# The guard, the input turns and the MLP's token shift of two windowed attention layers

## The reference

```python
def shift_token(t):                     # the second half of the features comes from the token before
    t1, t2 = jnp.split(t, 2, axis=-1)
    t2 = jnp.pad(t2, ((0, 0), (1, 0), (0, 0)))[:, :-1]
    return jnp.concatenate([t1, t2], axis=-1)
def l2norm(t):
    return t / jnp.clip(jnp.linalg.norm(t, axis=-1, keepdims=True), 1e-12)
def _layer(x, ...):
    q, k, v = split(shift_token(x) @ wqkv)            # 8 heads of 64
    q, k = rotary_xpos(l2norm(q) * qs, l2norm(k) * ksc)
    x = x + local_attention(q, k, v) @ wo             # windows of 64 tokens, each sees the one before too
    h = layernorm(shift_token(x)) @ w1 + b1
    a, g = jnp.split(h, 2, axis=-1)                   # 341 each
    return x + (a * gelu(g)) @ w2 + b2
```

## Time and profile before

| What | us |
|---|---|
| three executions | 1544.87, 1540.82, 1539.07; median 1540.82 |
| the profiled execution | 1543.41, its span 1541.6 |
| busy: PE, DVE, ACT, POOL | 1299.2, 1211.1, 946.1, 766.6 |
| `project` and `attend` | up to 610.8 |
| `mix` | 610.8 to 657.3 |
| `window`, layer 0 and 1 | 657.7 to 993.8; 1085.0 to 1423.8 |
| `mlp`, layer 0 and 1 | 994.3 to 1084.7; 1424.1 to 1514.9 |
| last norm | 1514.9 to 1541.6 |
| SP issues the 14 MLP loads, layer 0 | 660.57 to 670.63 |
| DVE L1368, first work of the first `mlp` | 994.29 |
| busy of the shift products L1258, L1259, L1260 | 10.8, 6.0, 10.3 |

### The profile page before, as it was taken

One profiled execution on the slowest core, in us unless ns is written; L12 is line 12 of the kernel. 1 busy time (PEld: TensorE's weight loads), 2 busy tenths in 40 slices (PEclk: granted clock), 3 DMA queues, 4 the chain that ended last, 5 costly groups with the idle time before them and its releaser, 6 DMA issues. The chain is left out here.

```text
span 1541.6 us, 30997 instructions
## 1 busy us (share of the span) xinstructions
PE 1299.2 (84%) x11013; PEld 741.1 (48%) x11013; DVE 1211.1 (79%) x2530; ACT 946.1 (61%) x2605; POOL 766.6 (50%) x742
## 2 busy tenths in 40 slices
PE   4389999999999997359999999699589999997892
PEld 2243444444444442326666666465266666665561
DVE  5576878787888770659999999666499999997667
ACT  4425776777677766747777777332377777775220
POOL 1001212221222121469999999310599999994102
PEclk9757999999999998679999999989799999999896
DMA  4412111111111101121111111000211111110001
GB/s 111 141 47 65 36 51 50 36 34 53 48 36 35 36 4 41 56 50 36 36 36 36 36 36 32 9 1 1 49 27 36 36 36 36 36 34 16 1 1 55
DMA packets 44272, 59.59 MB, mean 39 GB/s; under 512 B 8130, under 2 KB 31948, under 8 KB 41804
## 3 DMA queue, kind: packets, MB, share of 16 engines
q1 hardware_dynamic: 43544, 57.47, 13.8%
q10 hardware_dynamic: 576, 0.15, 0.0%
HBM read 26.67 MB, written 8.39 MB: 23 GB/s over the span
## 5 line engine op out<-in xcount | busy, mean ns | idle before, releaser
L593 DVE TENSOR_REDUCE a_nm<-a_psM 128x1 f32<-128x512 f32 (+3 forms) x768 | 375.1, 550 | 118.2 <-PE a_psM L429 65.8
L514 ACT ACTIVATE a_prob<-a_psE 128x512 f32<-128x512 f32 (+3 forms) x768 | 326.2, 491 | 161.7 <-PE a_psE L444 160.1
L1092 POOL TENSOR_TENSOR w_t<-w_raw,w_sin 128x256 f32<-128x256 f32 x256 | 264.1, 1060 | 49.6 <-ACT w_raw L1018 49.6
L429 PE MATMUL a_psM<-a_ks,a_qs 72*128 72x512 bf16 (+3 forms) x768 | 251.9, 346 | 18.3 <-PEq L76 18.1
L549 POOL TENSOR_SCALAR_AFFINE_SELECT a_prob<-a_prob 128x512 f32<-128x512 f32 x128 | 81.4, 637 | 371.9 <-ACT a_prob L514 371.9
L444 PE MATMUL a_psE<-a_qs,a_ks 84*128 84x512 bf16 (+3 forms) x768 | 253.2, 339 | 9.4 <-DMA a_qs<-a_nmT 5.8
L1041 ACT ACTIVATE w_prob<-w_psS,w_bias 128x128 f32<-128x128 f32 x512 | 181.4, 367 | 48.5 <-DVE w_bias L1169 48.4
L1102 POOL TENSOR_TENSOR w_rn<-w_ssm,mhalf 128x16 f32<-128x16 f32 x64 | 186.5, 2914 | 6.4
L458 PE MATMUL a_psO<-a_prob,v_all 128*32 128x512 f32 (+3 forms) x1536 | 170.1, 510 | 11.5 <-ACT a_oT L526 11.5
L444 PEld LDWEIGHTS a_psE<-a_qs,a_ks 84*128 84x128 bf16 x768 | 74.6, 99 | 188.5 <-ACT a_prob L514 118.2
L1097 POOL TENSOR_TENSOR w_rot<-w_t 128x1024 f32<-128x1024 f32 x64 | 152.1, 2376 | 8.8 <-issue 0.4
(11 more groups left out here) (139 smaller groups left out, 2509.9 us busy)
## 6 DMA issues: line engine op xcount, KB each, us to landing
w_vb<-w_v SPq DMA_DIRECT2D x128, 128.0 KB, 2.3
a_qs<-q_parts SPq DMA_DIRECT2D x16, 576.0 KB
a_ks<-k_parts SPq DMA_DIRECT2D x16, 576.0 KB
w_xc<-xf_sb SPq DMA_DIRECT2D x64, 64.0 KB, 2.0
q_parts<-p_parts SPq DMA_DIRECT2D x24, 128.0 KB
k_parts<-p_parts SPq DMA_DIRECT2D x24, 128.0 KB
out_x<-l_y SPq DMA_DIRECT2D x8, 256.0 KB, 2.3
a_qs<-a_nmT SPq DMA_DIRECT2D x32, 48.0 KB
```

Of the source, the lines that this page charges most:

```text
L429: mm = pe.matmul(out, qs[0:ROWS, g, j, i * P:(i + 1) * P], ks[0:ROWS, g, j, 512 * kc:512 * kc + n], start=True, stop=not diag)
L514: act.activation(prob[G % NPROB][:, j, 0:w], psE[:, r % NRING, 0:w], ACT.Exp, scale=SCALE0).then_inc(e_read, 1)
L593: dve.tensor_reduce(nm[:, s % 2, kc, i, j:j + 1], psM[:, r % MRING, 0:n], AX.X, ALU.max, negate=True).then_inc(m_read, 1)
L1092: i = pool.tensor_tensor(out[:, w, :, half, :], src[:, w, :, 1 - half, :], tab, ALU.mult)
```

## The change

In `mix` PE turns `o_tok` itself, and ACT's copy `stage` goes. In `window` PE turns the tile of `xf` itself and the `xc` loads go; the MLP weights are loaded after the spread of tile 7; the guard is a maximum over pairs (sum, 1e-24) by a reduction instead of a tensor-scalar maximum, for which `ss` gets a second column set once by a memset. In `mlp` the shift products go: SP transfers the second half of the features of `xf`, one partition and for partition 0 one tile on, into `back` before the stage's first work, two transfers a chunk, all issued at the start; DVE waits for a chunk's transfers before its statistics, and for the next chunk's before it overwrites `xf` in the residual.

```diff
@@ -712,11 +711,10 @@
             pe.wait_ge(w_in, 16)
 
             def turn(c, r):
-                at_least(pe, o_staged, 0, c, 1)
                 at_least(pe, oT_copied, 0, c, -1)
                 p = r % 2
                 for t in range(4):
-                    i = pe.transpose(psT[:, p, t * P:(t + 1) * P], oc[:, p, t, :], sb["ident"])
+                    i = pe.transpose(psT[:, p, t * P:(t + 1) * P], sb["o_tok"][:, c * 4 + t, :], sb["ident"])
                 i.then_inc(oT_done, 1)
 
             def project_out(c, r):
@@ -753,7 +747,7 @@
             def layers_input(c, r):
                 normal(1, c, r, lambda t: sb["xf"][:, c * 4 + t, :], lambda t: sb["x"][:, c * 4 + t, :], xf_done)
 
-            pipelined(act, NCH, 4, [(1, copy), (0, stage), (3, normal_a), (5, layers_input)])
+            pipelined(act, NCH, 4, [(1, copy), (3, normal_a), (5, layers_input)])
 
         @block.gpsimd
         def _(pool):
@@ -870,10 +862,6 @@
 
         @block.sync
         def _(sp):
-            def load_x(t, r):
-                at_least(sp, xT_done, base, t, -1)
-                sp.dma_start(xc[:, r % 2, :], sb["xf"][:, t, :]).then_inc(xc_in[r % 2], 16)
-
             def spread_v(t, r):
 
                 at_least(sp, v_copied, base, t, 1)
@@ -881,20 +869,18 @@
                 sp.dma_start(vb[r][0:WIN, :], v[r][0:WIN, :]).then_inc(vb_in[r], 16)
                 sp.dma_start(vb[(r + 1) % 4][WIN:P, :], v[r][WIN:P, :]).then_inc(vb_in[r], 16)
 
-            sp.wait_ge(zeroed, layer * 3 + 3)
-            for t in range(2):
-                load_x(t, t)
-            load_mlp_weights(nc, sp, io, sb, layer)
-            pipelined(sp, NT, 4, [(0, lambda t, r: None if isinstance(t, int) and t < 2 else load_x(t, r)), (2, spread_v)])
+            sp.wait_ge(zeroed, layer * 4 + 4)
+            for t in range(NT):
+                if t == 8:
+                    load_mlp_weights(nc, sp, io, sb, layer)
+                spread_v(t, t % 4)
 
         @block.tensor
         def _(pe):
             def turn_x(t, r):
-                p = r % 2
-                pe.wait_ge(xc_in[p], (base + t - p) * 8 + 16)
                 at_least(pe, pT_copied[0], base, t, -4)
                 at_least(pe, hT_copied, base, t, 0)
-                pe.transpose(psT[:, 0, 0:P], xc[:, p, :], sb["ident"]).then_inc(xT_done, 1)
+                pe.transpose(psT[:, 0, 0:P], sb["xf"][:, t, :], sb["ident"]).then_inc(xT_done, 1)
 
             def project_qk(t, r, w):
                 if w == 0:
@@ -1110,6 +1096,7 @@
             dve.memset(hT[WIN:P, 1, P:P + 1], 0.0).then_inc(zeroed, 1)
             dve.memset(kT[:, 1, :, :], 0.0).then_inc(zeroed, 1)
             dve.memset(vb[0][WIN:P, :], 0.0).then_inc(zeroed, 1)
+            dve.memset(ss[:, :, :, 1], 1e-24).then_inc(zeroed, 1)
 
             dve.wait_ge(w_in, WINDOW_LOADS)
             for w in range(2):
@@ -1132,11 +1119,11 @@
 
             def sums(t, r):
                 at_least(dve, sq_done, base, t, 1)
-                dve.tensor_reduce(ss[:, r % 2, :], sq[:, :].rearrange("p (h d) -> p h d", d=DH), AX.X, ALU.add).then_inc(ss_done, 1)
+                dve.tensor_reduce(ss[:, r % 2, :, 0], sq[:, :].rearrange("p (h d) -> p h d", d=DH), AX.X, ALU.add).then_inc(ss_done, 1)
                 at_least(dve, ss_done, base, t, 1)
                 at_least(dve, rn_done, base, t, -1)
 
-                dve.tensor_scalar(ssm[:, r % 2, :], ss[:, r % 2, :], 1e-24, None, ALU.max).then_inc(ssm_done, 1)
+                dve.tensor_reduce(ssm[:, r % 2, :], ss[:, r % 2, :, :], AX.X, ALU.max).then_inc(ssm_done, 1)
 
             def cosines(t, r):
                 at_least(dve, raw_done, base, t, 1)
@@ -1248,17 +1235,16 @@
 
         LOADS = 16 * 14
 
+        @block.sync
+        def _(sp):
+            for c in range(NCH):
+                t0 = c * 4
+                first = t0 if t0 % TB else t0 + 1
+                sp.dma_start(back[1:P, t0:t0 + 4, :], sb["xf"][0:P - 1, t0:t0 + 4, WIN:D]).then_inc(back_in[c], 16)
+                sp.dma_start(back[0:1, first:t0 + 4, :], sb["xf"][P - 1:P, first - 1:t0 + 3, WIN:D]).then_inc(back_in[c], 16)
+
         @block.tensor
         def _(pe):
-            def shift_half(c, r):
-
-                p = r % 2
-                at_least(pe, hn_done, base, c, -1)
-                out = psH[:, p, 0:4 * WIN].rearrange("p (t d) -> p t d", t=4)
-                pe.matmul(out, shift[:, :], sb["xf"][:, bass.ts(c, 4), WIN:D], start=True, stop=False, skip_group_check=True)
-                pe.matmul(out[:, 0, :], carry[:, :], last[:, c, :], start=False, stop=False, skip_group_check=True)
-                pe.matmul(out[:, 1:4, :], carry[:, :], sb["xf"][:, bass.ds(c * 4, 3), WIN:D], start=False, stop=True, skip_group_check=True).then_inc(shifted, 1)
-
             def turn(c, r):
                 at_least(pe, hn_done, base, c, 1)
                 at_least(pe, hT_done, base, c, 0)
@@ -1290,8 +1276,7 @@
                 i.then_inc(y_done, 1)
 
             pe.wait_ge(w_in, (layer + 1) * LOADS)
-            pe.wait_ge(last_set, (layer + 1) * 3)
-            pipelined(pe, NCH, 2, [(0, shift_half), (3, down), (1, turn), (2, up)])
+            pipelined(pe, NCH, 2, [(3, down), (1, turn), (2, up)])
 
         @block.gpsimd
         def _(pool):
@@ -1326,10 +1311,10 @@
         def _(dve):
             def statistics(c, r):
                 p = r % 2
-                at_least(dve, shifted, base, c, 1)
+                dve.wait_ge(back_in[c], (layer + 1) * 32)
                 for t in range(4):
                     dve.bn_stats(stats[:, p, t, 0, :], sb["xf"][:, c * 4 + t, 0:WIN])
-                    i = dve.bn_stats(stats[:, p, t, 1, :], psH[:, p, t * WIN:(t + 1) * WIN])
+                    i = dve.bn_stats(stats[:, p, t, 1, :], back[:, c * 4 + t, :])
                 i.then_inc(stats_done, 1)
                 at_least(dve, stats_done, base, c, 1)
                 carry_wait(dve, sb)
@@ -1360,16 +1345,16 @@
             def residual(c, r):
                 xs = sb["xf"][:, bass.ts(c, 4), :]
                 at_least(dve, y_done, base, c, 1)
+                if c + 1 < NCH:
+                    dve.wait_ge(back_in[c + 1], (layer + 1) * 32)
                 dve.tensor_tensor(xs, xs, psY[:, r % 2, :].rearrange("p (t n) -> p t n", t=4), ALU.add).then_inc(y_added, 1)
                 at_least(dve, y_added, base, c, 1)
                 dve.tensor_tensor(xs, xs, b2[:, :].unsqueeze(1).broadcast_to((P, 4, D)), ALU.add).then_inc(xf_done, 1)
 
 
-            dve.memset(last[:, :, :], 0.0).then_inc(last_set, 1)
-            dve.wait_ge(last_set, layer * 3 + 1)
-            src = sb["xf"].rearrange("p (b u t) n -> p b u t n", b=B, u=2)[:, :, 0, 3, WIN:D]
-            dst = last[:, 0:NCH, :].rearrange("p (b u) n -> p b u n", u=2)[:, :, 1, :]
-            dve.tensor_copy(dst, src).then_inc(last_set, 2)
+            for b in range(B):
+                dve.memset(back[0:1, b * TB, :], 0.0).then_inc(first_set, 1)
+            dve.wait_ge(first_set, (layer + 1) * B)
             dve.wait_ge(w_in, (layer + 1) * LOADS)
             pipelined(dve, NCH, 2, [(3, residual), (0, statistics), (2, gated), (0, norm)])
```

More of the change, by code:

```diff
@@ L683, in sem @@
             return ctx.enter_context(nc.semaphore("m_" + name))
-        oc = tile("m_oc", [P, 2, 4, P])
         ocT = tile("m_ocT", [P, 2, 4, P])
@@ L694, in mix @@
         psA = ctx.enter_context(nc.psum_tensor("m_psA", [P, 4, 512], F32))
-        w_in, o_staged, oT_done, oT_copied, a_done = sem("w_in"), sem("o_staged"), sem("oT_done"), sem("oT_copied"), sem("a_done")
+        w_in, oT_done, oT_copied, a_done = sem("w_in"), sem("oT_done"), sem("oT_copied"), sem("a_done")
         stats_done = [sem("stats_a"), sem("stats_x")]
@@ L736, in copy @@
                 act.activation(ocT[:, r % 2, :, :].rearrange("p t c -> p (t c)"), psT[:, r % 2, :], ACT.Copy).then_inc(oT_copied, 1)
-            def stage(c, r):
-                at_least(act, oT_done, 0, c, -1)
-                act.activation(oc[:, r % 2, :, :], sb["o_tok"][:, bass.ts(c, 4), :], ACT.Copy).then_inc(o_staged, 1)
             def normal(w, c, p, outs, ins, done):
@@ L825, in window @@
         cos, sin = tile("w_cos", [P, TB, 2, DH]), tile("w_sin", [P, TB, 2, DH])
-        xc = tile("w_xc", [P, 2, D])
         hT = tile("w_hT", [P, 2, P + 1])
         sq = tile("w_sq", [P, 2 * INNER])
-        ss, ssm, rn = tile("w_ss", [P, 2, 16]), tile("w_ssm", [P, 2, 16]), tile("w_rn", [P, 2, 16])
+        ss, ssm, rn = tile("w_ss", [P, 2, 16, 2]), tile("w_ssm", [P, 2, 16]), tile("w_rn", [P, 2, 16])
         raw = tile("w_raw", [P, 2, 2 * INNER])
@@ L847, in window @@
         w_in, tables, zeroed = sb["w_in"], sem("tables"), sem("zeroed")
-        xc_in = [sem("xc_in0"), sem("xc_in1")]
         vb_in = [sem(f"vb_in{r}") for r in range(4)]
@@ L1075, in slot @@
                     exps(s - 2, r2, 1)
-            act.wait_ge(zeroed, layer * 3 + 3)
+            act.wait_ge(zeroed, layer * 4 + 4)
             copy_hT(0, 0)
@@ L1121, in _ @@
```

(12 more changed lines are left out.)

## The result

The change gives 1529.4 us, median of four runs (1527.3 to 1531.2), against 1541.8 for the kernel before in the same session: ratio 0.992, interval 0.990 to 0.994. That is 12.5 us less (9 to 16). A second measurement in a later session (changed_again) gave 0.992 (0.990 to 0.994) again. The forecast was 1525.8, within 1507 to 1537, with a chance of 0.72 of more than 0.5% faster; 0.8% it is, inside the likeliest case's own range of 1516 to 1533.

A forecast was written before the change was run, and what follows sets the result against it. POOL was taken to bound the window layers, with DVE and POOL excluding each other for some forms. −27.8 − 4.4 − 0.4 + 0 + 17.6 = −15.0 from 1543.4 gives 1528.4, less 2.6 for the median: 1525.8 us, range 1507 to 1537.

The forecast's parts named there:

- the likeliest case: Whole kernel: the forecast itself, 1525.8 us, own range 1516 to 1533, chance 0.55.
- Part 1: Window layers: the guard as a reduction no longer waits for POOL, slots 9.15 instead of 9.63 us, −27.8 us.
- the early slot: Window layers before the change: a slot where DVE's cosine product ended before POOL's products, giving the forecast slot of 9.15 us.
- Rival C: Window layers: the DVE stall only moves to the copy within SBUF, only 0.14 a slot won; 1544.9 us, chance 0.10.
- Part 2: Turns straight from x: 2.2 us a layer at the window start, −4.4; mix stage without ACT's copies, −0.4.
- The copies at 0.4: Mix stage: removing eight ACT copies, mostly standing before waits, gains 0.4 us (bounds 0 and 5.1).
- Part 3: Steady MLP slots: removing PE's shift products gives 0, since waiting replaces the work and slots stay 9.38 us.
- Part 4: MLP start: first statistics wait for 127-row transfers through one DMA engine, 8.8 us a layer, +17.6 us.
- the rule that chunk 1 decides: MLP start: chunk 0's up stands behind chunk 1's turn on PE, so chunk 1's landing, 8.8 us late, sets the loss.
- the fixed part ahead of the pieces: MLP start: a shift transfer's time apart from its pieces, taken as 1.8 us from the xc load.
- B: MLP start: the shift transfers are spread and land in about 3 us, +1 each instead of 8.8; 1510 us, chance 0.12.
- D: MLP stage: a shift transfer lasts longer than a slot, 10.7 us, and paces the stage; 1555 us, chance 0.07.

The follow-up runs named there:

- guard_const_back: The changed kernel with the guard again a tensor with a constant, the rest of the change kept: 1558.0 us, ratio 1.010.
- guard_alone: The kernel before with only the guard's change (reduction over pairs, second column of ss and its memset): 1517.5 us, ratio 0.983.
- turns_alone: The kernel before with only the window turns taken straight from x and the MLP weights loaded after tile 7's spread: ratio 1.000.
- pe_shift_back: The changed kernel with the old MLP stage, the token shift by PE products again: 1509.2 us, ratio 0.978.
- half_width: The changed kernel with 128 instead of 256 bytes in each shift piece, leaving out the shift of the other 32 features: 1516.1 us, ratio 0.981.
- rows_126_and_1: The changed kernel with each shift transfer of 127 rows cut into one of 126 rows and one of 1: 1508.6 us, ratio 0.979.

## Why the prediction was right, and where it was off

**Part 1, −27.8.** From the second power to the last are 274.8 and 274.7 instead of 288.4 and 288.6: −13.6 and −14.0, so −27.6. The mechanism is shown by guard_const_back and guard_alone: the slot goes with the instruction's form, 9.64 or 9.15, whichever of the other parts is there. The value came from reading the early slot as a rehearsal of the new order. Rival C (only 0.14 a slot) is out: the copy L1149 is held, as said, but for 0.43 more than before where the guard saved 1.17, and DVE's cosine product still starts 1.28 before the power ends (median) and takes 1.22, so that it is through when POOL's products begin; these take 3.77.

**Part 2, −4.4 and −0.4.** From the first power to the second the gain is 2.2 and 2.6, where 2.2 each was worked out. This is shown as a local gain only; as a term of the time −4.4 isn't shown. Alone it is worth nothing (turns_alone, −0.6, between −3.2 and +1.9). Beside the guard it may be worth more: the window stages of pe_shift_back are 3.0 and 4.7 shorter than those of guard_alone. What goes with the difference is PE's clock at the stages' ends, which the forecast didn't look at; no run sets the clock by itself. In the changed kernel the first window stage gains 13.6 + 2.2 and gives back 0.5 before the first power and 0.9 behind the last, so 14.4; the second gains 14.0 + 2.6, and 0.4 net are given back at its ends. So of the 32.2 forecast for parts 1 and 2, 30.6 arrive; since the way from the last power to the MLP stage varies by 3.4 us from execution to execution and kernel to kernel, it is in part luck that the ends cost no more. The copies at 0.4 and the weights at 0 held, as far as 2 us can be told.

**Part 3, 0.** Held: MLP slots are 9.38 with and without the products, and 0.84 of waiting stands in their place.

**Part 4, +17.6.** Measured +19.2 (9.7 and 9.5). The engine count (one), the piece (14.4 ns against 14.3) and the transfer (7.3 us between chunks against 7.2) were right, and so was the rule that chunk 1 decides: its statistics come 9.4 late, and the first `up` product starts 9.3 late (22.5 after the opening instead of 13.2). It is 9.4 and not 8.8 mainly since the fixed part ahead of the pieces was longer (chunk 0 usable 9.4 after the opening instead of 9.0). The piece price was halfway between two sizes of another kind of transfer. At 256 bytes it was right, but at 128 the same line is 0.7 ns too high (half_width), so its precision here is partly luck. The rest, 0.3 in the first layer and 0.1 in the second, is a term that I had not set down: PE idles 15 us and then works at the lower clock for longer. The stretch at half grant is 23.8 us here,

```profile
980.30:1004.10 23.80, 5.69 (x13) 3.17 (x14) 8.38 (x56) 3.52 (x4) 2.80 (x6) 0.50 0.08 18
```

and 13.5 before,

```profile
996.80:1010.30 13.50, 8.21 (x24) 5.31 (x23) 8.34 (x55) 3.26 (x4) 3.63 (x6) 0.50 0.00 0
```

and the first twelve products `up` take 7.16 instead of 6.70, in the second layer 7.12 instead of 6.82. Rivals B (spread) and D (pacing the stage) are out; B's time, 1510, was nearly that of rows_126_and_1, where its condition is made true.

**Sum.** −15.0 was forecast; the stages give −11.4, the ratio −12.5 (−9 to −16). The difference is 1.6 in part 4, 1.6 in the window stages, where the ends gave back 1.8, and 0.4 in the copies, which the runs can't tell from nothing. The forecast of 1525.8 is 3.6 below the median.

## What to carry to other kernels

Where two engines exclude each other, look for small instructions that wait behind a large one, and ask whether another form of the same computation isn't held: here 0.19 instead of 1.35 on 16 numbers gave 5% of a slot and 4% of the stage. Before a shift by one partition is given to a transfer, count its rows: here a chunk of 127 rows took 7.3 us and one of 126 and 1 took 2.2, and either is free if it is issued while other work runs. A gain of 2 us at a stage's start should be called a gain only once the stage's end has been read.
